# Attention scores from split operands: 256 columns wide over both heads of a pair, with keys masked on GpSimd in place of queries on ScalarE

## What is computed

```python
H, D = 16, 256                       # heads, channels; 16 channels per head
pairs = [(0, 0), (1, 0), (1, 1)]     # (branch, offset): branch 0 takes every token,
                                     # branch 1 every second one from offset 0, then from 1
for br, off in pairs:
    r, S = DIL[br], 128              # segments of 128 tokens
    xs = x[:, off::r, :].reshape(b, -1, S, D)
    qkv = xs @ Wqkv[br].T + bqkv[br]
    scores = einsum('...qhd,...khd->...hqk', q, k) * 16 ** -0.5
    a = softmax(scores, axis=-1)
    o = einsum('...hqk,...khd->...qhd', a, v).reshape(..., S, D)
    outs.append(o @ Wout[br].T + bout[br])
result = sum(outs) / 3
```

## Time and profile before

| | |
|---|---|
| median of 3 runs | 4043.06 us |
| the profiled execution's own time | 4039.7 us |
| its span in the trace | 4037.8 us |
| mean granted TensorE clock | 0.984 of full |
| dilated attention in the span | about 1100 to 2206 us |
| its first and last scores (L1337) start at | 1137.7 and 2195.5 us |

### The profile page before, as it was taken

The page is one execution under the profiler, slowest core; times in us unless marked ns, Lnnn a source line. Parts: engine busy times, 40 slices in busy tenths (PEclk is TensorE's granted clock), DMA queues, the critical chain, the costliest instruction groups (busy, mean ns, idle before and its releaser), DMA issues. The chain is left out here.

```text
span 4037.8 us, 82429 instructions
## 1 busy us (share of the span) xinstructions
PE 3821.2 (95%) x29464; PEld 3342.0 (83%) x29464; DVE 3203.9 (79%) x7740; ACT 3070.6 (76%) x7818; POOL 2280.1 (56%) x1818
## 2 busy tenths in 40 slices
PE   7999999999889999999998799999999988999989
PEld 6888888888768888888887688888888877898878
DVE  7888888888668787878876788888888867756567
ACT  6888888888678888888886688888888867632166
POOL 7888888888611111111100788888888866512356
PEclk8999999999989999999999899999999998999999
DMA  2000000000010000000000200000000002331342
GB/s 65 16 17 17 17 17 17 17 17 17 21 37 12 23 13 23 12 23 12 23 7 12 70 17 17 17 17 17 17 17 17 17 16 93 124 101 58 123 147 89
DMA packets 135064, 141.99 MB, mean 35 GB/s; under 512 B 8672, under 2 KB 131968, under 8 KB 134656
## 3 DMA queue, kind: packets, MB, share of 16 engines
q1 hardware_dynamic: 134656, 136.71, 10.6%
HBM read 80.06 MB, written 56.62 MB: 34 GB/s over the span
## 5 line engine op out<-in xcount | busy, mean ns | idle before, releaser
L300 POOL TENSOR_TENSOR f_grid<-f_sim 128x1024 f32<-128x1024 f32 x512 | 968.5, 1908 | 0.0
L1483 ACT ACTIVATE a_ex<-a_p_s,a_mneg 128x128 f32<-128x128 f32 x2048 | 726.4, 408 | 149.9 <-DVE a_mneg L1537 149.9
L686 DVE SCALAR_TENSOR_TENSOR f_p_u<-f_grid,f_te,f_p_dot 128x1024 f32<-128x1024 f32 x512 | 652.9, 1275 | 112.6 <-PE f_p_dot L106 66.1
L308 POOL TENSOR_TENSOR f_q<-f_q 128x1024 f32<-128x1024 f32 x256 | 607.2, 2383 | 123.1 <-ACT f_q L558 120.6
L695 DVE SCALAR_TENSOR_TENSOR f_q<-f_p_u,f_rz,f_grid 128x1024 f32<-128x1024 f32 x512 | 650.5, 1270 | 0.4
L539 ACT ACTIVATE f_grid<-f_grid,f_negm 128x1024 f32<-128x1024 f32 x512 | 559.5, 1143 | 0.0
L1483 ACT ACTIVATION_READ_ACCUMULATOR a_ex<-a_p_s,a_mneg 128x1 f32 x2048 | 507.2, 248 | 0.0
L443 PE MATMUL f_p_y<-f_eup,f_wT 128*128 128x256 f32 x2048 | 472.9, 379 | 0.0
L438 PE MATMUL f_p_y<-f_wdn,f_hs 128*128 128x256 f32 x2048 | 468.3, 382 | 0.0
L443 PEld LDWEIGHTS f_p_y<-f_eup,f_wT 128*128 128x128 f32 x2048 | 388.6, 190 | 57.6
L438 PEld LDWEIGHTS f_p_y<-f_wdn,f_hs 128*128 128x128 f32 x2048 | 378.9, 190 | 49.5
(11 more groups left out here) (622 smaller groups left out, 10448.3 us busy)
## 6 DMA issues: line engine op xcount, KB each, us to landing
x_f<-f_yt SPq DMA_DIRECT2D x64, 256.0 KB, 2.2
f_xt<-x SPq DMA_DIRECT2D x32, 256.0 KB, 2.9
a_xt<-x_f SPq DMA_DIRECT2D x16, 512.0 KB, 3.9
x_a<-a_yt SPq DMA_DIRECT2D x16, 512.0 KB, 2.9
f_xt<-x_a SPq DMA_DIRECT2D x32, 256.0 KB, 2.9
c_xt<-x_f SPq DMA_DIRECT2D x16, 512.0 KB, 4.9
x_c<-c_yt SPq DMA_DIRECT2D x16, 512.0 KB, 3.2
b1p_xt<-x_c SPq DMA_DIRECT2D x16, 512.0 KB, 3.9
```

Of the source, the lines that this page charges most:

```text
L300: g_grid.mark(pool.tensor_tensor(grid[v][:, hd, :].rearrange("p (i j) -> p i j", i=XROWS), sx[:, hd, :].unsqueeze(2).to_broadcast([P, XROW ...
L308: g_pair.mark(pool.tensor_tensor(q[v][:, 2 * k, :], q[v][:, 2 * k, :], q[v][:, 2 * k + 1, :], ALU.add), f"{v}{k}")
L686: d_mask.mark(dve.scalar_tensor_tensor(out=p_u[:], in0=grid[v][:, hd, :], scalar=te[:, v, hd, TOP - 1:TOP], in1=p_dot[:], op0=ALU.is_ge, o ...
L1483: last = act.activation(ex[t.step % 2][:, i, n, :], p_s[i][:, n, :], ACT.Exp, bias=mneg[:, i, n:n + 1], accum_out=z[t.step % 2][:, i, n:n ...
```

## The change

Query and key are now both split into a high and a low float32r part. The two copies, each with one head zeroed, are made of the key instead of the query: `kz[br]` holds both copies side by side, so that one matmul covers both heads with 256 columns. Three products of parts replace one float32 product, so a unit has 2 x 3 x 4 = 24 matmuls of 256 columns in place of 16 of 128.

ScalarE writes every projection twice, once in float32 (`full`) and once rounded to float32r. GpSimd makes the low part, for the key also the four masked copies (high and low, e = 0 and 1), in a new function `split_qk`. It is issued in unit t for projection t + 5, in u = 2 behind `norm.root` and `scale`, in u = 7 ahead of `biased`. The first scores of a branch now wait for GpSimd (`g_qk`) and no longer for ScalarE. ScalarE waits for GpSimd's split of projection t - 2 before it overwrites `full`.

```diff
+        qT = [[m.sbuf(f"qT{br}{k}", DC, S, dt=F32R) for k in "hl"] for br in range(BR)]
+        kz = [[m.sbuf(f"kz{br}{k}", DC, 2, S, dt=F32R) for k in "hl"] for br in range(BR)]
+        full = [m.sbuf(f"full{k}", S) for k in range(2)]
+        k_hi, k_lo = [m.sbuf(f"k{k}h", S, dt=F32R) for k in range(2)], m.sbuf("kl", S, dt=F32R)
...
+                def split_qk(t):
+                    br, j = ur_of(t) // SEGS, t.step % SEGS
+                    c, x = j % DC, full[t.step % 2]
+                    a_qk.wait(pool, t)
+                    if j < DC:
+                        hi, lo = (a[:, c, :] for a in qT[br])
+                        g_qk.mark(pool.tensor_tensor(lo, x[:], hi.bitcast(F32), ALU.subtract))
+                        return
+                    hi = k_hi[t.step % 2]
+                    k_mark = Turn(t.group, t.step // SEGS * DC + j - DC, ROWS * UR // 2)
+                    g_qk.wait(pool, t - 1)
+                    g_kl.mark(pool.tensor_tensor(k_lo[:], x[:], hi[:].bitcast(F32), ALU.subtract))
+                    for n, part in enumerate((hi, k_lo)):
+                        if n:
+                            g_kl.wait(pool, k_mark)
+                        for e in range(2):
+                            last = pool.tensor_tensor(kz[br][n][:, c, e, :], part[:].bitcast(F32),
+                                                      par[:, e:e + 1].to_broadcast([P, S]), ALU.mult)
+                    g_qk.mark(last)
...
                 scale(first_row + 1)
+                pool.wait_ge(s_p, 16 * 4)
+                for j in range(AHEAD):
+                    split_qk(first_unit + j)
                 pool.wait_ge(s_b, 4)
                 biased(first_row)
...
                     if u == 2 and (r + 2).exists(last=rows):
                         norm.root(pool, r + 2)
                         scale(r + 2)
+                    if (t + AHEAD).exists(last=units):
+                        split_qk(t + AHEAD)
                     if u == 7 and (r + 1).exists(last=rows):
                         biased(r + 1)
...
                     if j == 0:
-                        a_qk.wait(pe, t + (SEGS - 1))
+                        g_qk.wait(pe, t + (SEGS - 1))
...
-                        for e in range(2):
+                        for n, (q, k) in enumerate(((0, 1), (1, 0), (0, 0))):
                             for i in range(QUAD):
-                                mm = pe.matmul(p_s[i][:, 2 * c + e, :], qz[br][lanes, c, e, j * P:(j + 1) * P],
-                                               kT[br][lanes, c, j * P:(j + 1) * P], start=True, stop=True)
+                                mm = pe.matmul(p_s[i][:, 2 * c:2 * c + 2, :], qT[br][q][lanes, c, j * P:(j + 1) * P],
+                                               kz[br][k][lanes, c, :, j * P:(j + 1) * P], start=n == 0, stop=n == 2)
...
                     c = j % DC
+                    if (t - 2).exists():
+                        g_qk.wait(act, t - 2)
                     if j < DC:
-                        for e in range(2):
-                            last = act.activation(placed(qz[br][:, c, e, :], br), natural(p_pr[:], br), ACT.Identity,
-                                                  bias=bqs[:, e, br, c:c + 1], scale=qs[:, e:e + 1])
+                        hi, bias, scale = qT[br][0][:, c, :], bqs[:, br, c:c + 1], HD ** -0.5
                     else:
-                        last = act.activation(placed(kT[br][:, c, :], br), natural(p_pr[:], br), ACT.Identity,
-                                              bias=bk[:, br, c:c + 1])
+                        hi, bias, scale = k_hi[t.step % 2][:], bk[:, br, c:c + 1], 1.0
+                    for out in (full[t.step % 2][:], hi):
+                        last = act.activation(placed(out, br), natural(p_pr[:], br), ACT.Identity, bias=bias, scale=scale)
                     a_qk.mark(last)
```

## The result

The changed kernel takes 4065.18 us (median of 5 runs, 4059.59 to 4066.06) against 4043.06 (5 runs, 4037.59 to 4046.23): the ratio is 1.005, its 95% interval 1.0038 to 1.0062. It is slower, by 22 us where 45 were forecast. The profiled execution's span is 4062.6 us against 4037.8, 24.8 more.

A forecast was written before the change was run, and what follows sets the result against it. A loop through ScalarE's exponentials, TensorE's transposes and VectorE's evictions was taken to bound the steady unit (8.31 us), not TensorE. Stalls 26 + clock 15 + opening 6 - scores 2 = +45 us, 4088; range 4048 to 4145.

The forecast's parts named there:

- The scores: Dilated attention's score matmuls on TensorE: 0.23 us less a unit, in steady units going into slack that grows to 0.45.
- The opening: Before the stage's first scores: two key splits on GpSimd delay them from 1137.71 to 1143.7, 6 us (4.4 to 7.7).
- The gain in units where the maximum waits: Last four units and seven of the first row, where VectorE's maximum waits for scores: 11 x 0.2 = 2 us gained.
- the clock term: Behind the stall TensorE's granted clock falls in half of 14 rows, 2.2 us each: 14 x 1.1 = 15 us.
- p: GpSimd's time for one key projection's five instructions: 5.5 us, ends 4.7 and 6.35.
- 2p - 8.7: Lateness of projection 7's split for the scores of u = 4: 2.3 us; 1.85 lost in 14 rows, 26 us.
- The handover: Projection 6 reaches GpSimd 1.37 us after u = 2 starts, at 1423.2; its split is reckoned from 1423.28.
- What is absorbed: Behind the stall before u = 4, the scores' slack of 0.45 us takes up part of the 2.3 late.
- Contention: Rival: GpSimd and VectorE hold each other up, p = 8.5, late 8.3; +173, 4216; chance 0.04.
- No overlap of the slots: Rival: the 24 float32r score matmuls run one by one, 2.9 us in place of 0.9; +225, 4270; chance 0.05.
- the splits are hidden: Rival: GpSimd needs 4.4 us or less per key projection, only the opening stays; +3, 4046; chance 0.07.
- TensorE is the bound: Rival: TensorE, 95% busy, bounds the kernel and splits are hidden; 128 x 0.23 = 29 less, 4018; chance 0.07.

The follow-up runs named there:

- extra1: Changed kernel plus one dead GpSimd instruction of about 1 us in u = 2, between the norm and the split of projection 7; 4089.23 us, 1.0115.
- opening: Changed kernel with VectorE making three of the four masked copies of projections 2 and 3 before the loop; 4064.51 us, 1.0058 of the kernel before.
- late2_all: Changed kernel with root and scale started early, seven of eight `turn_h` behind the second maximum, and VectorE making three of four opening masked copies; 4028.23 us, 0.9952.
- scale_early: Changed kernel with means and `norm.root` moved to u = 1 and `scale`'s first three pieces waiting only for part 5; 4043.26 us, 1.0005 of the kernel before.
- one_product: Changed kernel with only the high by high product in the scores, 8 matmuls a unit in place of 24; 4057.65 us, 1.0039 of the kernel before.
- turn_late_after: Changed kernel with all of VectorE's `turn_h` moved behind its second maximum; 4059.59 us, 1.0044 of the kernel before.
- turn_late_before: Kernel before the change with all of VectorE's `turn_h` moved behind its second maximum; 4067.91 us, 1.0065.
- extra3: Changed kernel plus one dead GpSimd instruction of about 3 us in u = 2, between the norm and the split of projection 7; 4128.77 us, 1.0219.

## Why the prediction was off by half

**Right.** The direction and the place were right: there is one stall in each row that prepares a norm, at u = 4, released by GpSimd's masked low key. The scores are worth nothing in a steady unit. ScalarE's second write costs nothing: the wait of its exponentials for the maximum is still there, 101.0 us against 104.9. The opening was forecast at 6 and measured 6.6. The gain in units where the maximum waits was forecast at 2; in the last two rows nine units are 0.18 to 0.20 shorter, and the rows 1.4 in all.

**The step that failed is the clock term, 14 x 1.1 = 15 us, and the size of the stall on which it rests.** I counted 1.1 us in each of 14 rows, a loss of 2.2 in every second one. In the 13 regular rows the granted clock stayed at 1.00 behind the stall, and that unit took 8.01 us (in one row 8.06). Only the first row, with a stall of 2.91, has a slow unit behind it (9.47). So the term measured about 1.5 us in place of 15. It was not wrong in kind: in extra1, at stalls a little above the 2.3 I forecast, the clock fell in five of 13 rows, and a fall cost mostly 1.5, not 2.2. It was applied to a stall that came out at 1.61 late, 1.54 idle, and at that length no run shows a fall at this place.

**Why the stall was shorter: 26 us forecast, 17 measured.**
- *The five instructions.* I took p = 5.5 for a key projection; it is 1303.66 - 1298.40 = 5.26. The groups by form over the whole span:

```profile
L1293 POOL TENSOR_TENSOR a_kz1l<-a_kl,a_par 128x512 fp32r<-128x512 f32 x64 | 65.2, 1039 | 0.0
...
L1288 POOL TENSOR_TENSOR a_kl<-a_full,a_k0h 128x512 fp32r<-128x512 f32 x32 | 41.3, 1289 | 218.0 <-ACT a_k0h L1496 218.0
```

A subtraction with two full operands costs 1.29. The estimate of 1.12 that I drew from the Trainium skill, GPSIMD Engine Reference, section 3.1, was too low for it and, taken for all five, too high in sum (5.6 against 5.26). The product with one spread column costs 1.04, as the spread one in the earlier trace rows did (1.069), and each instruction starts about 0.04 before the recorded end of the last. Since the term is 2p - 8.7, the 0.24 count twice: 0.5.
- *The handover.* The split of projection 6 starts 1298.40 - 1297.14 = 1.26 after u = 2 instead of 1.44 (1423.28 less 1421.84): ScalarE's two writes, started at 1296.93 and 1297.52 and 0.81 long each, take 1.40 together where the old pair of the query took 1.57. That is 0.2 more.
- *What is absorbed.* I expected 0.45, and 0.31 came back. This went the other way, by 0.15 us a row.

In sum 2.3 - 0.5 - 0.2 = 1.6, less 0.3, in 13 rows: 17 us. I had counted 14 rows; the first one nets 0.7, and this is luck: its stall and the slow unit behind it cost more than any other row's, but a slow unit of the kernel before is missing.

**The rivals.** Contention: there is none in the loop, where p = 5.26 and `scale` takes 4.85 as before (4.84); it shows in the runs opening and late2_all, where VectorE too reads both operands from SBUF. (The sum of this rival charged 1.4 us for projection 11, 1.5 late; less the 0.45 absorbed it is 1.1, and its 4216 becomes about 4211.) That elementwise work belongs on VectorE (the Trainium skill, GPSIMD Engine Reference, section 4.1 Engine selection) did not decide the case: scale_early keeps all of this work on GpSimd and loses nothing in the loop. The factor of about two stated there no run here can show, since VectorE has the product only beside a busy GpSimd. No overlap of the slots: the second group of four starts 0.22 behind the first, the others 0.11 to 0.12 apart, and VectorE gets the scores 1.01 us after they begin behind a stall, where it took 1.16; one by one at 0.12 they would need 2.9. So the matmuls run four at a time. The Trainium skill, TensorEngine Tiling, Key Properties, says that tiles operate independently; the trace agrees, for float32r as well. That the splits are hidden is refuted by the stall. That TensorE is the bound is refuted by one_product, where 16 of 24 matmuls are gone and the unit is unchanged.

**What remains of the change's gain.** It is real and was hidden twice, behind VectorE's `turn_h` and behind GpSimd's queue. With both out of the way a row is 65.66 - 64.83 = 0.83 us shorter than with the old scores and `turn_h` moved alike. The time differs by 8 us in the medians (4023.28 against 4031.59), with the opening still 7 us later.

## What to carry to other kernels

Before a stall is priced from a queue, each instruction in it wants its own row, and the penalty that comes on top (here the clock) depends on the stall, so it must be priced again at each end of the stall's range and not carried over from the middle. Work added to an engine that idles half of the time (the changed kernel's GpSimd is busy for 451 of the 877 us from 1203 to 2080) costs by its place in the queue: find what stands between the handover and the deadline, and what that in turn waits for, before adding or moving anything. A gain on an engine that is 95% busy can be worth nothing until the evictions that hide it are moved; test that by removing most of the work, and before moving an instruction look who needs its result. Work moved to an idle engine can slow the engine it came from, as in the opening.

## What the hardware showed that I had not expected

- Two stalls of TensorE of equal length, 2.51 and 2.52 us, with the same work around them, were followed by a full clock once and by a lowered one the other time; the loss is 1.4 to 1.5 us in most cases, 2.8 in one of extra1's. Behind TensorE's wait of 1.90 us in turn_late_after it came in 11 of 15 rows, more often than behind 2.5 us in extra1, and behind the same wait in turn_late_before in five of 15. So the length alone does not tell; what else does was not tried.
- On GpSimd a power of 4 elements on each partition took 1.03 us, as much as a product of 512 with a spread column (1.04); of 16 elements it took 2.92 (extra3).
- GpSimd's subtraction of 512 elements took 1.80 and its product 1.37, in place of 1.29 and 1.04, while VectorE ran products from SBUF beside it (opening).
